# Two expert layers with their logits and exponential table inside the norm, and residual norms whose last group VectorE finishes

## The reference, cut to what matters

```python
def routed_ffn(x, router_w, w1, w2):              # "L1_ffn": 8 experts, top 2
    probs = sigmoid(x @ router_w.T)
    topw, sel = top_k(probs, 2); topw = topw / (topw.sum(-1, keepdims=True) + 1e-20)
    y = relu(x @ W1[e])**2 @ W2[e]                # for every expert e
    return sum over the two chosen e of topw * y

def null_attention(x, context, ...):              # "L2_xattn"
    ...
    out = out @ Wout
    return (out - mean) * rsqrt(var + 1e-6) * ln_scale + ln_bias

def last_ffn(x, ...):                             # "L3_ffn"
    y1 = _ln(x + _mha(x, ...), ln1_g, ln1_b)
    gates = softmax(y1 @ wg); idx = argmax(gates) # one of 8 experts, at most 256 tokens each
    moe = gate * ((y1 @ w1[e] + b1[e]) @ w2[e] + b2[e])   # 0 for a token that finds no room
    return _ln(y1 + moe, ln2_g, ln2_b)
...
x = x + last_ffn(layernorm(x), ...)               # the program's output
```

## Time and profile before

| | us |
|---|---|
| median of 3 runs | 2350.74 (2348.56 to 2352.39) |
| profiled execution | 2351.17 |
| its span | 2349.3 |
| TensorE busy | 2057.0 |
| VectorE busy | 1252.7 |
| ScalarE busy | 1019.3 |
| GpSimd busy | 300.4 |
| mean granted TensorE clock | 0.959 of 2.4 GHz |

### The profile page before, as it was taken

One profiled execution on the slowest core, in us unless ns is written; L12 is line 12 of the kernel. 1 busy time (PEld: TensorE's weight loads), 2 busy tenths in 40 slices (PEclk: granted clock), 3 DMA queues, 4 the chain that ended last, 5 costly groups with the idle time before them and its releaser, 6 DMA issues. The chain is left out here.

```text
span 2349.3 us, 38236 instructions
## 1 busy us (share of the span) xinstructions
PE 2057.0 (88%) x14629; PEld 1545.4 (66%) x14629; DVE 1252.7 (53%) x2505; ACT 1019.3 (43%) x2851; POOL 300.4 (13%) x392
## 2 busy tenths in 40 slices
PE   6789998899997689979999999978998998785795
PEld 4556666566665589766666667657886777663684
DVE  6457665788876144365554455655444555553113
ACT  3247774777775245333333333443222544333122
POOL 0101110222211524200000000031002000001212
PEclk8989999999999889989999999999999999997898
DMA  3000001121212633340000000010002000005352
GB/s 132 18 1 1 1 2 46 28 56 38 58 33 90 234 85 90 99 148 10 10 10 10 1 10 1 1 32 1 1 1 79 28 19 22 1 1 167 126 184 81
DMA packets 92564, 114.79 MB, mean 49 GB/s; under 512 B 20217, under 2 KB 75521, under 8 KB 91489
## 3 DMA queue, kind: packets, MB, share of 16 engines
q1 hardware_dynamic: 87440, 98.75, 13.8%
q0 software_dynamic: 4944, 13.59, 1.6%
HBM read 79.89 MB, written 25.08 MB: 45 GB/s over the span
## 5 line engine op out<-in xcount | busy, mean ns | idle before, releaser
L957 ACT ACTIVATE ca_prob<-bank,ca_nmax 128x512 f32<-128x512 f32 x256 | 174.2, 691 | 73.2 <-DVE ca_nmax L1024 73.2
L1024 DVE TENSOR_REDUCE ca_nmax<-bank 128x1 f32<-128x512 f32 x256 | 164.2, 683 | 40.9 <-PE bank L806 40.9
L957 ACT ACTIVATE na_prob<-bank,na_nmax 128x257 f32<-128x257 f32 x256 | 118.1, 474 | 148.4 <-DVE na_nmax L1024 148.4
L820 PE MATMUL bank<-cst,ca_prob 128*128 128x128 f32 x1024 | 140.6, 278 | 7.6 <-DVE ca_pT L1030 5.9
L820 PEld LDWEIGHTS bank<-cst,ca_prob 128*128 128x128 f32 x1024 | 111.0, 141 | 53.6 <-issue 44.9
L957 ACT ACTIVATE ra_prob<-bank,ra_nmax 128x256 f32<-128x256 f32 x256 | 118.4, 486 | 53.4 <-DVE ra_nmax L1024 53.4
L1024 DVE TENSOR_REDUCE na_nmax<-bank 128x1 f32<-128x257 f32 x256 | 90.9, 418 | 68.7 <-PE bank L806 68.7
L2267 PE MATMUL bank<-sf_h,sf_W 128*128 128x512 f32 x512 | 120.1, 395 | 0.0
L2267 PEld LDWEIGHTS bank<-sf_h,sf_W 128*128 128x128 f32 x512 | 95.9, 187 | 23.5
L2135 PE MATMUL bank<-na_Wkv,na_cxT 128*128 128x512 f32 x224 | 103.6, 605 | 0.0
L1024 DVE TENSOR_REDUCE ra_nmax<-bank 128x2 f32<-128x512 f32 x128 | 82.0, 683 | 39.6 <-PE bank L806 39.6
(11 more groups left out here) (475 smaller groups left out, 4611.9 us busy)
## 6 DMA issues: line engine op xcount, KB each, us to landing
xl_w<-in_L_ffn_w SPq DMA_DIRECT2D x16, 1024.0 KB, 7.6
rf_sent<-rf_w SPq DMA_DIRECT2D x13, 390.0 KB, 6.2
rf_xin<-rf_sent SPq DMA_DIRECT2D x39, 128.0 KB, 2.1
dp_cx<-in_ctx_tok SPq DMA_DIRECT2D x4, 1024.0 KB, 13.8
ca_v<-in_ctx_values SPq DMA_DIRECT2D x8, 512.0 KB, 4.8
rf_W<-in_L_ffn_w SPq DMA_DIRECT2D x8, 512.0 KB, 10.6
rf_rows<-rf_back SPq DMA_DIRECT2D x8, 512.0 KB, 5.6
na_Wkv<-in_L_xattn_Wkv SPq DMA_DIRECT2D x1, 4096.0 KB
```

Of the source, the lines that this page charges most:

```text
L820: mm = pe.transpose(TB[f % 2][:, j * P:(j + 1) * P], prob[:, n % 2, u, c0:c0 + P], ident)
L957: e = act.activation(prob[:, n % 2, u, hh * keys:(hh + 1) * keys], S[u][:, hh * keys:(hh + 1) * keys], ACT.Exp, bias=nmax[:, n % 2, u, hh: ...
L1024: v.tensor_reduce(nmax[:, n % 2, u], S[u][:, 0:W].rearrange("p (h k) -> p h k", h=per), AX.X, ALU.max, negate=True).then_inc(maxed, 1)
```

## The change

- In the two norms with `resid`, GpSimd first adds `shift` to the last group of the residual. VectorE finishes that group itself, with two instructions (scaled x gain + residual) after its last scaling; ScalarE's map and GpSimd's adds for it are gone.
- The logits of both expert layers are made in the norm's hook at NG: those of groups 0 to 2 first, those of group 3 when it is ready.
- In these two norms ScalarE loads the exponential's table after the last root, by a dummy activation; in the last layer this stands ahead of the last group's map.
- Last layer: `back` is cleared at the start of the block after the norm, and GpSimd waits for it only before it sends results there; the exponential stands one row copy earlier.
- Both layers: `meta` is loaded after the first two loads of rows.

```diff
@@ layer_norm_phase
                     for gi in range(NG):
-                        sp.wait_ge(added, KD * (gi + 1))
+                        if gi == NG - 1:
+                            sp.wait_ge(added_last, KD)
+                        else:
+                            sp.wait_ge(added, KD * (gi + 1))
                         sp.dma_start(part(feature_rows(store), gi), part(dst, gi)).then_inc(stored, 16)
...
                 if resid is not None:
-                    for gi in range(NG):
+                    last = part(resid, NG - 1)
+                    for k in range(KD):
+                        po.tensor_scalar(last[:, k], last[:, k], shift[:, k:k + 1], None, ALU.add).then_inc(shift_added, 1)
+                    for gi in range(NG - 1):
                         for k in range(KD):
                             po.wait_ge(shifted, KD * gi + k + 1)
...
+            if table is not None:
+                act.wait_ge(table_set, 1)
+                act.activation(g.hold[:], eps[:], table).then_inc(table_set, 1)
             if gain is not None:
-                affine(NG - 1)
-                act.wait_ge(shifted, KD * NG)
+                if resid is None:
+                    affine(NG - 1)
+                act.wait_ge(shifted, KD * (NG if resid is None else NG - 1))
...
             v.wait_ge(scaled, NG)
+            if resid is not None:
+                v.wait_ge(shift_added, KD)
+                for k in range(KD):
+                    v.scalar_tensor_tensor(part(dst, NG - 1)[:, k], g.ln_cent[:, NG - 1, k], gain[:, k:k + 1],
+                                           part(resid, NG - 1)[:, k], ALU.mult, ALU.add).then_inc(added_last, 1)
+                v.wait_ge(added_last, KD)
@@ routed_ffn_layer
-        layer_norm_phase(g, "n1f", prefetch=prefetch, prepare=prepare)
+        def early(pe, at, scaled, rooted, centred, shifted):
+            if at == NG:
+                pe.wait_ge(router, 16)
+                for some in (range(NG - 1), (NG - 1,)):
+                    pe.wait_ge(scaled, some[-1] + 1)
+                    for k in range(KD):
+                        for gi in some:
+                            mm = pe.matmul(g.bank[0][32 * gi:32 * gi + 32, :], Wr[:, k], g.XN[:, k, gi * GT:(gi + 1) * GT],
+                                           start=(k == 0), stop=(k == KD - 1), skip_group_check=True)
+                mm.then_inc(logits, 1)
+        layer_norm_phase(g, "n1f", prefetch=prefetch, prepare=prepare, early=early, table=ACT.Exp)
...
                 sp.wait_ge(sent_all, 16 * 2 * TT)
-                sp.dma_start(meta[:], sent[:, D:RW].rearrange("(t p) d -> p t d", p=P)).then_inc(meta_in, 16)
                 for i in range(NT):
...
                     sp.dma_start(xin[:, i % 4], sent[i * P:(i + 1) * P, 0:D]).then_inc(ldx[i % 4], 16)
+                    if i == 1:
+                        sp.dma_start(meta[:], sent[:, D:RW].rearrange("(t p) d -> p t d", p=P)).then_inc(meta_in, 16)
...
-                pe.wait_ge(router, 16)
-                for k in range(KD):
-                    for gi in range(NG):
...
-                mm.then_inc(logits, 1)
@@ expert_layer, prefetch
-                for n in range(T // (4 * P)):
-                    sp.dma_start(back[...], zero[:, :, 0:D]).then_inc(zs, 16)
+            def early(pe, at, scaled, rooted, centred, shifted):
+                if at == NG:
+                    pe.wait_ge(wl, 48)
+                    pe.wait_ge(centred, NG)
+                    for some in (range(NG - 1), (NG - 1,)):
+                        for k in range(KD):
+                            pe.wait_ge(shifted, KD * some[-1] + k + 1)
...
+                    mm.then_inc(lp, 1)
@@ expert_layer, sync
+                    for n in range(T // (4 * P)):
+                        sp.dma_start(back[...], zero[:, :, 0:D]).then_inc(emptied, 16)
                     sp.wait_ge(sent_all, 16 * TT)
-                    sp.dma_start(meta[:], ...).then_inc(meta_in, 16)
                     load_rows(sp, 0)
                     load_rows(sp, 1)
+                    sp.dma_start(meta[:], ...).then_inc(meta_in, 16)
 @@ expert_layer, gpsimd
-                    po.wait_ge(zs, 16 * 2 * (T // (4 * P)))
+                    po.wait_ge(zs, 16 * (T // (4 * P)))
...
                     po.wait_ge(addressed, 4)
+                    po.wait_ge(emptied, 16 * (T // (4 * P)))
@@ expert_layer, tensor
-                    pe.wait_ge(wl, 48)
-                    for k in range(KD):
-                        for gi in range(NG):
...
-                    mm.then_inc(lp, 1)
@@ expert_layer, scalar
-                        if q == 5:
+                        if q == 4:
                             act.wait_ge(st, 3)
                             act.activation(pe8[:], dif[:], ACT.Exp).then_inc(eg, 1)
```

More of the change, by code:

```diff
@@ L2641, in expert_layer @@
             yt = sb("yt", [P, 2, 2, D])
[L2642 to L2643 removed]
+            wl, made, zeroed, zs, emptied, held, sent_all, blank = (g.sem("xl_" + n) for n in (
+                "weights", "made", "zero_made", "zeroed", "returns_zeroed", "held", "rows_sent", "gate_blank"))
             ldw = [g.sem(f"xe_weights{j}") for j in range(2)]
@@ L2691, in prepare, with early @@
                 po.wait_ge(numbered, 2)
-            norm(prefetch, prepare)
+            def early(pe, at, scaled, rooted, centred, shifted):
+                if at == NG:
[4 more added lines that the diff above has]
+                            pe.wait_ge(shifted, KD * some[-1] + k + 1)
+                            for gi in some:
+                                mm = pe.matmul(g.bank[0][32 * gi:32 * gi + 32, :], Wg[:, k], g.XN[:, k, gi * GT:(gi + 1) * GT],
+                                               start=(k == 0), stop=(k == KD - 1), skip_group_check=True)
+                    mm.then_inc(lp, 1)
+            norm(prefetch, prepare, early)
             with nc.Block() as block:
```

33 lines of the change are left out of this document (13 added, 20 removed).

## The result

| | before | after |
|---|---|---|
| median of the runs of this comparison | 2349.65 us (4 runs) | 2333.45 us (4 runs, 2332.99 to 2334.55) |
| ratio | | 0.9931, interval 0.9915 to 0.9947 |
| profiled execution, its span | 2351.17, 2349.3 | 2333.39, 2331.5 |
| mean granted clock | 0.959 | 0.964 |

The change is faster by 16.2 us (0.7%), where 11.35 were forecast; 2333.45 lies just under the lower end of the range (2334.0). Over all sets of this study the kernel before has a median of 2347.8 us (100 executions, 2340.4 to 2354.3, three disturbed ones left out), the changed kernel 2333.5 (16 executions, 2329.9 to 2339.9): 14.4 us.

What follows compares the result with a forecast made beforehand. At the four edited places TensorE mostly idles, waiting for chains on other engines. Gains 3.70 + 1.6 + 4.55 + 1.5 = 11.35 us, taken from 2350.74, gave 2339.4 us; range 2334 to 2345.

Steps and rivals of the forecast that it cites:

- the mark of 9: Routed layer, sign of failure: over 9 us from the last row transfer's landing to the first hidden product, then 8.
- part 4: Last expert layer: early logits and table, later clearing bring the first row transfer 4.55 us earlier (3.1 plus 1.45).
- Part 1: Two residual norms: last group finished on VectorE gains 1.85 us each, 3.70 together.
- Part 2: Routed layer: logits and table load in the norm bring the first row transfer 2.7 us earlier.
- rival A: Both expert layers: last group's logits at half clock, 3.64 instead of 1.94 us, total 2342.8; chance 0.15.
- Part 3: Routed layer: `meta` behind two row loads delays the first hidden product, loss 1.1 us (bounds 0.4 and 2.8).
- Rival B: Routed `meta` costs 2.8 instead of 1.1 us, late clearings delay first row transfers by 2; total 2343.1; chance 0.10.
- Part 5: Last layer: rows loaded before `meta` reach TensorE sooner, gain 1.5 us.
- Rival D: Tile loops: earlier restart meets the clock badly, 32 us longer at half clock, 2355.4 us or more; chance 0.01.
- Rival C: Last layer's norm: a table load keeps ScalarE for 2.66 us, last map 1.1 later, total 2340.5; chance 0.04.
- theory 3: Set up after the result, for TensorE: the clock's steps are tied to the program; untouched distances repeat within 0.5 us.

Runs made afterwards that it cites:

- p1: Kernel before with only the two residual norms' last group finished on VectorE: 2341.51 us, ratio 0.9972.
- p3: Kernel before with only the last expert layer's edits (logits, table, clearing, `meta` behind rows, earlier exponential): 2342.35 us, ratio 0.9974.
- c0: The kernel before, run again unchanged: 2347.94 us, ratio 0.9995.
- r0: Kernel before with only the last layer's clearing of `back` moved behind the barrier: 2346.16 us, ratio 0.9991.
- p2: Kernel before with only the routed layer's edits (logits and table in the norm, `meta` behind two row loads): 2347.68 us, ratio 0.9999.
- q1: Changed kernel with the routed layer's `meta` loaded ahead of its rows again: 2335.97 us, ratio 0.9951 to the kernel before.
- r1: Changed kernel with `meta` ahead of the rows again in the last layer alone: 2335.55 us, ratio 0.9939 to the kernel before.
- q3: Changed kernel without the early table load in the last layer's norm: 2336.09 us, ratio 0.9952 to the kernel before.
- r2: Changed kernel with routed `meta` first and idle matmuls (30 and 10 routed, 22 last layer): 2346.28 us, ratio 0.9991 to the kernel before.
- t1: Changed kernel with routed `meta` first and idle matmuls (one lot of 22 routed, 12 last layer): 2328.28 us, ratio 0.9914 to the kernel before.

## Why the prediction was wrong

The direction and the order of the waits were right: each announced mark of the profile was found (VectorE before TensorE's next phase, the routed and the last layer's first row transfer early, no table load in either block, the last layer's first row transposes 2.8 us after the row load's issue), and of the four signs of failure (half clock under the early logits, a late map, over 9 us to the routed hidden product, a slower pace of transfers) one was just crossed: 9.2 us from the landing of the last row transfer (SP's next issue, 818.89) to the routed layer's first hidden product (828.05), where it had been 8. That is 1.2 more, and 1.1 was its price, so the mark of 9 was set too low.

The size failed, in two places. Between the two first profiles lie 17.8 us. Of these the edited stretches gave 14.2 (2.1 routed, 1.9 null, 8.2 last, 2.0 final), where I had summed 11.35; the other 3.7 are in *rest*, where nothing was edited. The first is a term of the sum that was too small, in part 4. The second is luck of the executions that I took for base. Either one put right would have left 2333.45 inside the range: with 2.2 more in part 4 its lower end is 2331.8, with the pooled median for base 2331.1.

- **Part 1**, 3.70 forecast, 3.9 measured. The instruction costs 0.71 us, not 0.75.
- **Part 2**, 2.7 forecast. 3.2 against the first profile, 1.6 against an execution whose logits had full clock. About right for the profile, too much for the kernel as a whole: I priced the edit from a state that p1 and p3 had too, but c0 and r0 hadn't. The logits themselves took 1.9 at full clock, as assumed, so rival A falls; the barrier cost 0.3, not 0.5.
- **Part 3**, loss 1.1 forecast, 0.8 to 1.1 measured (first step on `meta` 8.0 to 8.3 us after the last row transfer instead of 7.2). Rival B falls: its 2.8 wasn't seen, nor a delay of the first row transfers.
- **Part 4**, 4.55 forecast, 6.7 against the first profile (37.8 to 31.1), 6.3 against c0. **This is the step that failed**: "ScalarE's two maps deliver the halves at 2146.87 and 2147.57", and with it "Its first row transposes, now at 2152.51, move to 2149.40: 3.1 us". Those transposes came 28.0 us after the norm's start in the first profile and come 22.9 after it now, so this term is 5.1; from them to the first row transfer it went from 9.8 to 8.2, 1.6 where 1.45 were forecast. I kept the norm as the profile had it, with half clock in its first 4 us and its last map 22.2 us after its start. At full clock that map comes at 20.5. In the kernel before this brings nothing, since SP holds the barrier until 23.0 to 24.0 us after the start and the logits behind it still take 3.64 (p1, p2: 38.3 and 38.5 to the first transfer, with the map at 20.5; before, c0: 37.8 and 37.4, with the map at 22.2). With the clearing moved and the logits in the norm nothing is left to wait for, and the 1.7 us count. q1 shows the other side: the same edits behind a norm with half clock reach 32.8, a gain of 5.0 from 37.8, close to my 4.55. What a faster norm triggers I had not asked.
- **Part 5**, 1.5 forecast, 1.5 measured (r1 against the changed kernel).
- **Base.** 2350.74, the median of three runs, lies 2.9 us above the median of 100. One kernel spreads over 14 us, where I had allowed two, so the lower end 2334.0 was too high by this alone. With 2347.8 for base the same sum gives 2336.5, 3.0 over the pooled 2333.5.

Against that went a small loss that I had named but not summed: the last layer's loop is 116.5 to 116.7 us instead of 115.3 to 116.1. It starts at half clock all the same. Rival D has this mechanism, at a price of about 1 us instead of 16. Rival C falls with q3.

The edited stretches account for most of the pooled lead, not for all: in the three profiles of the changed kernel they are together 12.7 us shorter than the mean of before, c0 and r0 (181.8 less 169.1), and the pooled medians differ by 14.4. The remaining 1.7 us are about what the choice of profiled executions would make. Those of before, c0 and r0 took 2344.4 us on average, 3.4 below the pooled median, at mean granted clocks of 0.959, 0.963 and 0.963, where 96 executions of the kernel before average 0.960; among these, 0.001 more clock goes with about 1.2 us less. Those of the changed kernel took 2333.4, which is its median. A clock that suits the changed kernel outside the edited stretches, as theory 3 would have it, isn't seen in the profiles: *rest* holds 108, 96 and 96 us at half clock in before, c0 and r0, and 110, 105 and 100 in the three profiles of the changed kernel. Inside *last* it is 41 to 42 us against 29. What stays open is why the last norm starts at half clock in some executions (before, c0, r0, q1) and not in the others; the same kernel was never profiled in both states.

## What to carry to other kernels

Before a wait is taken away, ask at which clock the engines ahead of it ran in the profile, and what they will do at the other: an edit that frees a barrier from SP also lets through every gain ahead of it that SP had hidden. Read small edits off distances between events in the profile, since the total of a 2.3 ms kernel moved by 14 us on its own. Take the base from many executions and not from three. Where TensorE waits some 20 to 30 us ahead of a long loop, matmuls with no use that end as the data land made each of two loops 1.3 to 2.7 us shorter; too long a lot costs more than that (r2).

## What the runs showed of the hardware

- Both tile loops start at a granted clock of 0.50 after TensorE has idled (28.9 us in the last layer of the changed kernel), and at 1.00 when idle matmuls fill the time before (t1). How much of a phase runs low differs between executions of one kernel: the same sixteen routed logits took 3.34 us or 1.92 (c0), and the first profile's *rest* took 8.3 us more than c0's. The Trainium skill, "TensorE: Matmul & The Clock Gate", Part 1, states that the transition varies from run to run; the trace agrees.
- A wait of one engine can hide the clock of another: half clock in the first 4 us of the norm moved its last map by 1.7 us (22.2 to 20.5), and behind SP's clearing issues the first row transfer came no earlier for it (37.4 and 37.8 us with half clock, 38.3 and 38.5 without).
- `meta`, in pieces of 8 or 16 bytes, is small but holds up what follows: the rows right behind it reached TensorE 1.5 us (last layer, r1) to 2.9 us (routed, q1) later, and it was itself used 0.8 to 1.1 us later for standing behind two row loads.
- A 512-column idle matmul in f32 took 0.87 us at full clock (30 of them 25.99 us, in 60 records, r2): it shows as two records.
